# A two-stage transformer kernel: one-pass masked maxima, the last sums on VectorE, and the first routed rows in another order

## The reference, cut to what matters

```python
x = x + slots                                   # what the kernel calls x1
xn = layernorm(x)                               # "final norm"
scores = xn @ w_router;  idx = top_k(scores, 256)
x_sel = xn[idx];  h = rmsnorm(x_sel, g1)
q, k, v = h @ W_qkv.T                           # 16 heads of 32
att = q @ k.T / sqrt(32);  att[upper triangle] = -inf
att = softmax(att);  o = att @ v                # 256 x 256 for each head
x_attn = o @ W_out.T
x_ff = (silu(h2 @ W1.T) * (h2 @ W2.T)) @ W3.T   # h2 = rmsnorm(x_sel + x_attn, g2)
out = x + xn;  out[idx] = x[idx] + x_sel + x_attn + x_ff
```

## Time and profile before

| | |
|---|---|
| median of three runs | 2345.51 us |
| profiled execution, its own time | 2347.54 us |
| its span | 2345.8 us |
| PE busy | 2304.2 us, 98% of the span |
| DVE busy | 1592.5 us, 68% |
| ACT busy | 976.6 us, 42% |
| POOL busy | 1002.4 us, 43% |
| mean granted clock of TensorE | 0.993 |

### The profile page before, as it was taken

How to read it: one execution, slowest core, us unless ns; L and a number is a source line. 1 busy time by engine, 2 the same in 40 slices (tenths; PEclk the granted TensorE clock), 3 DMA queues, 4 the chain that set the end, 5 groups by cost and what they waited for, 6 DMA issues and landing times.

```text
span 2345.8 us, 30910 instructions
## 1 busy us (share of the span) xinstructions
PE 2304.2 (98%) x11541; PEld 1892.6 (81%) x11541; DVE 1592.5 (68%) x2904; ACT 976.6 (42%) x1650; POOL 1002.4 (43%) x1353
## 2 busy tenths in 40 slices
PE   8999999999999999999999999999999999999998
PEld 4888888888888888888888888888888887777886
DVE  7777666757577584778757667785775768875642
ACT  2565433333333333333333433334333345766432
POOL 1566235152453525435454452554535257753200
PEclk9999999999999999999999999999999999999999
DMA  5587000000052000013400001250000012104330
GB/s 202 178 305 271 14 1 1 1 1 1 36 182 97 5 23 5 15 50 126 153 6 14 14 5 59 108 171 5 10 19 1 19 46 90 69 32 138 101 112 19
DMA packets 87125, 158.58 MB, mean 68 GB/s; under 512 B 10801, under 2 KB 33337, under 8 KB 83134
## 3 DMA queue, kind: packets, MB, share of 16 engines
q1 hardware_dynamic: 82838, 150.26, 18.6%
q0 software_dynamic: 2688, 6.31, 0.9%
q10 hardware_dynamic: 1450, 0.04, 0.0%
HBM read 106.21 MB, written 50.37 MB: 67 GB/s over the span
## 4 chain that ended last, share of the span: by engine, by line
PE 79%; DVE 10%; POOL 6%; ACT 2%; issue 2%; DMA 1%; ACTq 0%; SPq 0%; DVEq 0%; POOLq 0%
PE ps L222 24%; PE ps L224 24%; PE ps L223 24%; PE ps L1511 3%; DVE moments L2012 3%; POOL gT1l L2637 2%; DVE slots L2410 1%; DVE tbuf L2397 1%; DVE zTl L2053 1%; DVE tbuf L2404 1%; PE ps L1667 1%; PE ps L449 1%; DVE mx L2357 1%; ACT prob L1915 1%; PE ps L1496 1%
## 5 line engine op out<-in xcount | busy, mean ns | idle before, releaser
L222 PE MATMUL ps<-zTh,kTl 128*128 128x512 f32 (+1 forms) x912 | 332.3, 364 | 2.8 <-ACT prob L1915 2.2
L224 PE MATMUL ps<-zTh,kTh 128*128 128x512 f32 (+1 forms) x912 | 324.6, 356 | 0.0
L223 PE MATMUL ps<-zTl,kTh 128*128 128x512 f32 (+1 forms) x912 | 324.3, 356 | 0.0
L222 PE MATMUL ps<-vh,prob_lo 128*128 128x512 f32 x768 | 306.1, 399 | 0.0
L224 PE MATMUL ps<-vh,prob_hi 128*128 128x512 f32 x768 | 300.1, 391 | 0.0
L223 PE MATMUL ps<-vl,prob_hi 128*128 128x512 f32 x768 | 299.3, 390 | 0.0
L2535 POOL TENSOR_SCALAR rs_m<-mv_m 128x1 f32<-128x1 f32 x96 | 55.5, 578 | 542.3 <-DVE mv_m L2014 540.7
L2053 DVE TENSOR_TENSOR zTl<-ps,zTh 128x512 fp32r<-128x512 f32 x224 | 151.3, 683 | 193.0 <-ACT zTh L1780 192.8
L1915 ACT ACTIVATE prob<-ps,nb 128x1024 f32<-128x1024 f32 x96 | 107.3, 1118 | 252.7 <-DVE nb L2362 252.2
L1762 ACT ACTIVATE zbuf<-slots,rs_m 128x512 f32<-128x512 f32 x96 | 78.4, 816 | 303.6 <-POOL rs_m L2540 303.6
L222 PEld LDWEIGHTS ps<-zTh,kTl 128*128 128x128 f32 x912 | 172.0, 189 | 35.0 <-DVE zTl L2053 7.1
(11 more groups left out here) (332 smaller groups left out, 5697.9 us busy)
## 6 DMA issues: line engine op xcount, KB each, us to landing
ctx<-in_ctx_dram SPq DMA_DIRECT2D x8, 1024.0 KB, 7.5
slots<-in_x_dram SPq DMA_DIRECT2D x8, 1024.0 KB, 6.6
kT_d<-kTh SPq DMA_DIRECT2D x6, 1024.0 KB, 7.9
kT_d<-kTl SPq DMA_DIRECT2D x6, 1024.0 KB, 9.9
s_d<-slots SPq DMA_DIRECT2D x6, 1024.0 KB, 5.1
v_d<-vh SPq DMA_DIRECT2D x6, 1024.0 KB, 8.7
v_d<-vl SPq DMA_DIRECT2D x6, 1024.0 KB, 11.8
kTh<-kT_d SPq DMA_DIRECT2D x3, 2048.0 KB, 10.5
```

Of the source, the lines that this page charges most:

```text
L222: nc.tensor.matmul(out, ll, rh, start=start, stop=False)
L223: nc.tensor.matmul(out, lh, rl, start=False, stop=False)
L224: return nc.tensor.matmul(out, lh, rh, start=False, stop=stop)
```

## The change

Four things change, all in the routed phase.

1. `masked_max` becomes four tensor_tensor_reduce, one for each head and row tile: (scores + mask) * -QS is written and its minimum kept in `nmax`. The minimum of the negated values is the negated maximum, so ACT's exponential takes scale -1. `masked_ready` is given after the last of the four, and `nmax_ready` is gone: both PE and ACT wait for `masked_ready`.
2. `last_x1` moves from POOL to DVE, each tile's sum just ahead of its moments: tiles 0 and 1 ahead of the loop, the others at i = 1, 2, 3 of batch 0.
3. Order on DVE: `gathered_stats(1)` ahead of `masked_max(0)`; `gathered_stats(2)` from i = 3 to i = 5; `score(0..2)` at i = 4. Order on POOL: the scatters 2 to 7 of batch 2 behind `normalise(2)` and `normalise(3)`, `gather(2)` from i = 0 to i = 3, `row_scale(2)`, `row_rms(2)` from i = 3 to i = 5, `final(k)` earlier. Order on ACT: `exps(0)`, `exps(1)`, `exps(2)` one place later, `norm_gathered(2)` at i = 5, `final_norm` pairs at i = 2, 3, 4, 7 in place of 2, 3, 5, 6, and `norm_gathered(3)` ahead of `exps(21)` in place of behind `keep(18)` and `o_hi(8)`.
4. V(0, 0) waits for each low part of its weights alone, not for all four ahead of the first product.

```diff
         def V(q, t):
             bank_free(("V", q, t))
-            pe.wait_ge(sem("w_split"), 2 + 2 * C)
             for c in range(C):
+                if (q, t) == (0, 0):
+                    pe.wait_ge(sem("w_split"), 2 + C + c + 1)
...
         def exps(n):
-            act.wait_ge(sem("nmax_ready"), 2 * n + 2)
+            act.wait_ge(sem("masked_ready"), n + 1)
...
-                    A.activation(prb[n % 4][:, g, cs], prb[n % 4][:, g, cs], ACT.Exp, bias=nmax[:, h, t:t + 1],
+                    A.activation(prb[n % 4][:, g, cs], prb[n % 4][:, g, cs], ACT.Exp, bias=nmax[:, h, t:t + 1], scale=-1.0,
                                  accum_out=psums[:, h, t:t + 1]).then_inc(sem("pexp_ready"), 1)
...
+        qk_out(0, 5); qk_out(0, 6)
         exps(0)
-        qk_out(0, 5); qk_out(0, 6)
+        qk_out(0, 7)
         exps(1)
-        qk_out(0, 7)
         norm_gathered(1)
-        exps(2)
         act.wait_ge(sem("tr_h"), QT)
         norm_rows(1)
-        v_out(0, 0); v_out(0, 1)
+        v_out(0, 0)
+        exps(2)
+        v_out(0, 1)
...
+            if q == 2 and i == 2:
+                norm_gathered(3)
             if rows_out:
                 exps(n + 3)
...
-                if i == 4:
+                if i == 5:
                     norm_gathered(2)
...
-                if i in (2, 3, 5, 6):
-                    k = (2, 3, 5, 6).index(i)
+                if i in (2, 3, 4, 7):
+                    k = (2, 3, 4, 7).index(i)
                     final_norm(2 * k); final_norm(2 * k + 1)
...
-            m_ = prb[n % 4][:, :, :]
-            V.scalar_tensor_tensor(m_, ps[:, 0:2, 0:3 * P], QS,
...
+            for g in range(2):
+                for t, cs in enumerate((slice(0, P), slice(P, 3 * P))):
+                    last = V.tensor_tensor_reduce(prb[n % 4][:, g, cs], bank(g)[:, cs], mask[:, cs], -QS, -NEG,
+                                                  ALU.add, ALU.min, nmax[:, 2 * i + g, t:t + 1])
+            last.then_inc(sem("masked_ready"), 1)
...
+        gathered_stats(1)
         masked_max(0)
-        gathered_stats(1)
         masked_max(1)
...
         masked_max(2)
-        dve.wait_ge(sem("row_in"), 3 * 16)
-        final_stats(B - 1, 0)
         invert(1)
+        last_x1(0); last_x1(1)
...
+                if i in (1, 2, 3):
+                    last_x1(2 * i); last_x1(2 * i + 1)
+                if i == 4:
+                    score(0); score(1); score(2)
+                if i == 5:
                     gathered_stats(2)
...
-        last_x1(0, 1)
         row_scale(1); row_rms(1)
-        scatter(B - 2, range(2, 5))
         normalise(0)
         normalise(1)
-        scatter(B - 2, range(5, NT))
-        last_x1(2, 3)
+        final(0)
...
                 if i == 0:
+                    scatter(B - 2, range(2, 5))
+                if i == 1:
+                    scatter(B - 2, range(5, NT))
+                    final(1)
+                if i == 2:
+                    final(2)
+                if i == 3:
                     pool.wait_ge(sem("tok_in0"), 2 * 16)
                     gather(2)
-                    final(0)
...
+                    final(3)
+                if i == 5:
                     row_scale(2); row_rms(2)
...
+            def last_x1(j):
+
+                dve.wait_ge(sem(f"x_in{j // 4}"), (HS // 2 + B) * 16)
+                dve.wait_ge(sem("slots_ready"), ALL_TILES - NT + j + 1)
+                V.tensor_tensor(stg_l[:, j, :], stg_l[:, j, :], slots[:, j, :], ALU.add).then_inc(sem("x1_ready"), 1)
+                final_stats(B - 1, j)
```

More of the change, by code:

```diff
@@ L801, in routed_act @@
             if q == 2 and i == 2:
-                norm_gathered(3)
                 act.wait_ge(sem("tr_h2"), QT)
@@ L889, in routed_dve_early, with routed_dve @@
         return queries_lo, gathered_stats, h_lo
-    def routed_dve(dve, gathered_stats, h_lo, final_stats, scores, count_tokens, rank_tokens):
+    def routed_dve(dve, gathered_stats, h_lo, last_x1, scores, count_tokens, rank_tokens):
         V = nc.vector
@@ L903, in masked_max @@
                 dve.wait_ge(sem("turned"), n - 3)
-            m_ = prb[n % 4][:, :, :]
-            V.scalar_tensor_tensor(m_, ps[:, 0:2, 0:3 * P], QS,
-                                   mask[:, :].rearrange("p (o k) -> p o k", o=1).to_broadcast([P, 2, 3 * P]),
-                                   ALU.mult, ALU.add).then_inc(sem("masked_ready"), 1)
-            dve.wait_ge(sem("masked_ready"), n + 1)
-            for t, cs in enumerate((slice(0, P), slice(P, 3 * P))):
-                V.tensor_reduce(nmax[:, 2 * i:2 * i + 2, t], m_[:, :, cs], AX.X, ALU.max, negate=True)\
-                    .then_inc(sem("nmax_ready"), 1)
+            for g in range(2):
[3 more added lines that the diff above has]
+            last.then_inc(sem("masked_ready"), 1)
         def o_lo(c):
@@ L1029, in routed_dve @@
             if q == 0:
-                if i == 0:
-                    final_stats(B - 1, 1)
-                if i == 1:
-                    final_stats(B - 1, 2); final_stats(B - 1, 3)
-                if i == 2:
-                    final_stats(B - 1, 4); final_stats(B - 1, 5)
-                if i == 3:
-                    gathered_stats(2)
-                    score(0)
-                if i == 4:
-                    final_stats(B - 1, 6)
-                    score(1); score(2)
-                if i == 5:
-                    final_stats(B - 1, 7)
+                if i in (1, 2, 3):
[3 more added lines that the diff above has]
+                if i == 5:
+                    gathered_stats(2)
                     score(3)
@@ L1170, in routed_pool_early, with routed_pool @@
         return gather, row_scale, row_rms, make_mask, rstd_two
-    def routed_pool(pool, rstd_two, gather, row_scale, row_rms, last_x1, base, scatter):
+    def routed_pool(pool, rstd_two, gather, row_scale, row_rms, base, scatter):
         G = nc.gpsimd
@@ L1218, in routed_pool @@
                 if i == 0:
+                    scatter(B - 2, range(2, 5))
[5 more added lines that the diff above has]
+                if i == 3:
                     pool.wait_ge(sem("tok_in0"), 2 * 16)
                     gather(2)
-                    final(0)
-                if i == 1:
-                    last_x1(4, 5)
-                    final(1)
-                if i == 2:
-                    last_x1(6, 7)
-                if i == 3:
-                    final(2)
+                    final(3)
+                if i == 5:
                     row_scale(2); row_rms(2)
-                if i == 5:
-                    final(3)
             if q == 1:
@@ L2512, in _ @@
                 slot_round(g, g == B * ROUNDS - 1)
-            routed_dve(dve, gathered_stats, h_lo, final_stats, scores, count_tokens, rank_tokens)
+            routed_dve(dve, gathered_stats, h_lo, last_x1, scores, count_tokens, rank_tokens)
         @block.gpsimd
@@ L2731, in slot_round @@
                 rstd_z(6); rstd_z(7)
-            def last_x1(*tiles):
-                for j in tiles:
-                    pool.wait_ge(sem(f"x_in{j // 4}"), (HS // 2 + B) * 16)
-                    pool.wait_ge(sem("slots_ready"), ALL_TILES - NT + j + 1)
-                    G.tensor_tensor(stg_l[:, j, :], stg_l[:, j, :], slots[:, j, :], ALU.add).then_inc(sem("x1_ready"), 1)
             def base(b, j):
@@ L2748, in _ @@
                 slot_round(g, g == B * ROUNDS - 1)
-            routed_pool(pool, rstd_two, gather, row_scale, row_rms, last_x1, base, scatter)
+            routed_pool(pool, rstd_two, gather, row_scale, row_rms, base, scatter)
 _NAMES = {
```

## The result

The changed kernel takes 2341.85 us (median of 20 runs, 2337.11 to 2347.31), the kernel before on the same chips 2346.68 (20 runs, 2344.78 to 2350.92). The ratio is 0.9977, 95% interval [0.9971, 0.9983]: 5.4 us faster by the ratio, 4.8 by the two medians, where 8.9 were forecast. The profiled execution took 2341.60 us with a span of 2339.9, 5.9 less than before; PE is busy for 2301.5 us of it, VectorE for 1575.8, ACT for 975.6, POOL for 990.0, and the mean granted clock is 0.994.

The account below looks back on a forecast made before the run. PE sets the pace, with POOL, ACT and DVE in turn late behind its waits. Gains of 10.1 us, less 0.3 and 0.9, make 8.9 off the 2345.5 us median: 2336.6 us, range 2333 to 2342.

Parts of the forecast that it names:

- 6 to 11: Whole kernel: the forecast case, a gain of 6 to 11 us, chance 0.66.
- 0 to 5: Whole kernel: the case that half the gain is taken back, a gain of 0 to 5 us, chance 0.18.
- instruction count decides: Masked maxima on DVE: four instructions with accumulator reads take 3.1 us a pair, not 1.93; 2349 us; chance 0.06.
- (a): Up to `scores(3)`: PE waits longer ahead of `scores(1)`, then runs without a gap; 4.1 us earlier, 1.6 later if clock falls.
- (b): From `scores(3)` to `scores(12)`: POOL's normalisations come early, ACT's late `score(7)` limits; `scores(12)` 6.9 us earlier in all.
- (c): From `scores(12)` to `scores(14)`: DVE still late for `scores(13)`; 12.3 us in place of 12.72, gain 0.4.
- (d): From `scores(14)` to `I()`: one-pass maxima let DVE finish `place` in time; PE's 1.40 us wait goes.
- (e): Pairs 18 to 20: earlier `norm_gathered(3)` removes PE's 1.12 us wait and 0.3 of the 1.73.
- (f): Deductions: 0.3 us for banks freed 0.25 later at each remaining wait, 0.9 for a clock fall after the idle around `S()`.
- ACT and DVE take back half: Routed phase: contended sums on DVE, maxima at 1.4 us, two clock falls; gain 3 to 4.5, 2341.5 us; chance 0.18.
- the order of `score(6)`, `(7)` costs more: ACT ends them 3 us later, `S()` and `masked_max(11)` slide; gain 6 us, inside the range, no chance of its own.
- no longer full between 1990 and 2020: Sign on POOL's timeline: POOL was to have free time between 1990 and 2020 us.

Follow-up runs that it names:

- d1: Kernel after with `norm_gathered(2)` on ACT at i = 6, behind `exps(9)`, in place of i = 5; 2340.64 us, 0.9967 of before.
- a3: Kernel after with `final_norm(6)`, `(7)` on ACT at i = 5, ahead of `norm_gathered(2)`, in place of i = 7; 2338.91 us, 0.9966 of before.
- a4: Kernel after with `gather(2)` on POOL at i = 2 and `final(2)` at i = 3; 2342.58 us, 0.9979 of before.
- b1: Kernel after with `masked_max(0)` on VectorE ahead of `gathered_stats(1)` again; 2341.41 us, 0.9964 of before.
- c1: Kernel after with four moves: `masked_max(0)` ahead of `gathered_stats(1)`, earlier `gather(2)`, `final_norm(6)`, `(7)` at i = 5, `norm_gathered(2)` at i = 6; 2333.16 us, 0.9935 of before.
- f2: Kernel after with `norm_gathered(3)` back behind `keep(18)` and `o_hi(8)`; 2343.28 us, one execution.
- b2: Kernel after with `masked_max(0)` ahead of `gathered_stats(1)`, earlier `gather(2)`, and `final_norm(6)`, `(7)` at i = 5, `norm_gathered(2)` staying at i = 5; 2333.75 us, 0.9946 of before.
- a1: Kernel before with the one-pass masked maxima alone; 2342.46 us, 0.9985 of before.
- f1: Kernel after with V(0, 0) waiting for all four low parts of its weights again; 2342.33 us, one execution.
- f3: c1 with the two-pass masked maxima of before; 2339.67 us, 0.9965 of before.

## Why the prediction was right in kind and 3 us off in size

The median of 2341.85 us lies 0.15 us inside the right end of the range, 2333 to 2342; that it fell inside is in part luck, since the runs spread over 10 us. The gain of 5.4 us falls between two of the cases that were given chances (6 to 11, and 0 to 5) and so in neither. The steps, one by one:

- **The one-pass form** was priced at 1.2 us (1.1 to 1.4); it takes 1.16. The banks and the maxima come as put. "The new form does not occur in this trace" was a misreading: the line of the earlier trace rows is the same call, tensor_tensor_reduce, at 512 columns (693 ns), and gave the price of a long instruction with accumulator directly. POOL's neighbourhood doesn't touch it: over all 128 operations the longest took 423 ns, with POOL 88 to 92% busy between 2000 and 2020, and 27 of them ran beside one of POOL's wide products or sums. The Trainium skill ("GPSIMD Engine Reference", section 1) has the contention for instructions with two SBUF inputs, and the trace agrees: the four `wo_lo`, which have two, took 0.95 to 1.76 us. The rival "instruction count decides" needed 0.6 us for each of the four and got 0.29 and 0.42. The Trainium skill ("VectorE: DVE Perf Modes", section "The TRN2 errata — SBUF-src ops pay a fixed extra latency per instruction") gives `(N+151)/0.96` ns for an fp32 tensor_tensor; as an estimate for the new instructions that is 291 and 424 ns, and the trace agrees (286 and 419). The advice of the same page (section "Rules for kernel authors") to minimise the count of operations would have kept three instructions of 1.93 us in place of eight of 1.16; here the measurement decides against it.
- **`last_x1` on VectorE** was put at 6 us, at most 12; it took 6.5 (808 ns each).
- **(a)** The gain to `scores(3)` was put at 4.1 us, or 2.5 should the clock fall behind the 2.1 us wait. The wait came as 2.22, the clock fell, the gain is 3.01; with no fall (d1) it is 4.5, with a longer one (a3, a4) 1.4. The step held, and its size hangs on the clock; that the maximum stood behind the moments was taken for cheap and costs 1.3 us at full clock, 2.8 with the fall (b1).
- **(b) is the step that failed.** It was to bring 2.8 us from `scores(3)` to `scores(12)` and brought -0.2. The prediction put `gather(2)` near 2005 and let ACT start on `norm_gathered(2)` at 2014. The gather was issued from 2008.86 on, for the six scatters took 0.97 to 1.34 us each where 1.01 was put, and 1.18 us for one instruction of `final(1)` and 2.05 for two of `normalise(5)` stand ahead of it. Its rows landed at 2014.34, and the scales came at 2018.6: 4.6 us late on ACT. From there the replay was right: it allowed 11.5 us from that start to `score(7)`; the trace has 2018.62 to 2029.60, 11.0. PE's waits between `scores(3)` and `scores(12)` sum to 6.0 us where 2.5 were put. a3 shows that the last norms' place carries the waits around `S()`: with the gather as late as ever it brings 2.7 of the 3.0 us that were missing. a4 shows that the gather alone does not help, and c1 that the four moves together were worth 5.2 us in this stretch.
- **(c)** was put at 12.3 us and is 13.21: the clock was at 0.50 from 2031.2 to 2034.6, and two `wo_lo` beside POOL's sum (1.73 us from 2032.46) took 2.63 us together, ahead of the maximum for which `scores(13)` waits.
- **(d)** put at 1.4 us, measured 1.64, and borne out by the ten kernels at 27.0 us and the four with the two-pass form. **(e)** put at 1.4, measured 2.03; f2 gives 1.46 for the move itself, and the rest is that the clock was at 0.50 from 2078.5 to 2081.9 before and full after. **(f)** had 0.3 for banks that come free later: the stretch behind `scores(24)` is 0.11 longer. Its 0.9 was for one fall of the clock; a second came, the one at 1976, which (a) had named as a case.
- The sum forecast was 4.1 + 2.8 + 0.4 + 1.4 + 1.4 - 1.2 = 8.9, for (a) to (f); by stretches the trace has 3.01 - 0.18 - 0.49 + 1.64 + 2.03 - 0.11 = 5.90, and the runs 5.4. That is the number of the rival "ACT and DVE take back half" (2341.5), and its two clock falls came (1976 and 2031) with ACT at 10.00 of 10 from 2020 to 2030; but neither the sums nor the maxima were dear, as it had them. Nearest was the rival "the order of `score(6)`, `(7)` costs more": it had ACT 3 us later than worked out, `S()` and `masked_max(11)` sliding with it, and a gain of 6. ACT was 4 us later. What this rival doesn't name is what made ACT late: one late gather, with three queues standing for it in turn. That is read from the timelines; no run with the early gather alone gained by it.
- Of the signs named, POOL "no longer full between 1990 and 2020" was wrong (8.43, 9.18 and 8.79 of 10): the scatters filled the room that the sums had left, and that was the hint at (b) which the prediction didn't follow up.

Why `scores(0)` moves by 5 us between executions with the same code up to there can be read from the same windows. Every profile shows the clock at 0.50 near 30 us, and all but b2's near 85 us. Up to `scores(0)` b2 lost 1.7 us of full clock, a1 and f2 3.4, before, d1, f1 and f3 5.1, the seven others 6.8; their `scores(0)` stand at 1965.8, at 1967.5 and 1968.0, at 1968.5 to 1969.5, and at 1969.5 to 1970.7. The spread of the runs goes with the clock too. Of the 20 runs of the kernel after, the two with a mean granted clock of 0.991 took 2345.19 and 2347.31 us, the seven with 0.994 from 2341.60 to 2343.03, the one with 0.997 took 2337.11. At one and the same clock, here 0.995, a kernel's runs lie within 2 us, and before, after and c1 stand apart:

| kernel | runs with 0.995 | us |
|---|---|---|
| before (beside the experiments) | 13 | 2343.64 to 2345.60 |
| after | 2 | 2339.87 and 2339.91 |
| a3 | 3 | 2337.25 to 2338.91 |
| f3 | 2 | 2339.67 and 2339.95 |
| b2 | 1 | 2335.62 |
| c1 | 2 | 2334.31 and 2334.51 |

So c1's gain over the kernel after (5.5 us here, two runs each) is not a lucky clock. What stays open is what decides in an execution whether the clock falls at a given wait. Between `scores(0)` and `scores(31)` c1 had no fall, b2 one stretch, and the others two to four, at different places.

## What to carry to other kernels

When an item moves in one queue, follow its product through every queue to the last reader, with the time at which each queue would stand for it: here one gather issued late made DVE, ACT and PE stand 3.3, 3.8 and 2.3 us, each with unrelated work behind. A single move that gains nothing doesn't clear such a chain: a4 took away PE's 1.79 us and got 2.61 elsewhere. Alone the four moves gave 0.13, 0.11, 0.10% and nothing, with intervals as wide as these gains, together 0.42%; only the sum is shown, and whether they pay more together than one by one is not. c1 without the early gather was not run. Before comparing two profiles, sum the clock that each has lost. And an instruction count says little: eight short instructions with the reads hidden beat three long ones by 0.77 us a pair.
